# A pipelined convolution, attention and mixture-of-experts kernel: transposes of z moved on TensorE, rank sums from 5 products in place of 14

## The reference, cut to what matters

```
x = x + conv(_gn(x))          # a 7x7 filter per image and channel, made from the image: keys, softmax,
                              # 1x1 conv, layer norm, relu, 1x1 conv; then the depthwise convolution
t = tokens(x)                 # (16, 256, 128)
z = _ln_t(t)
q = tanh(z);  a = softmax(q q^T / sqrt(128));  t = t + a z
z2 = _ln_t(t)
probs = softmax(z2 router_w + router_b);  the best 2 of 8 experts per token
t = t + sum over the 2: prob * expert(z2)       # 128 -> 256 -> gated 256 -> 128
```

## Time and profile before

| | |
|---|---|
| Median of 3 runs | 386.15 us (382.89 to 387.73) |
| Profiled execution, its own time | 386.41 us |
| Its span | 384.6 us |
| TensorE busy in the span | 302.8 us (79%) |
| VectorE, ScalarE, GpSimd busy | 236.7, 132.4, 164.2 us |
| Mean granted TensorE clock | 0.87 of full speed |
| First phase, to the end of GpSimd's last row DMA | 239.9 us |

### The profile page before, as it was taken

How to read it: one execution, slowest core, us unless ns; L and a number is a source line. 1 busy time by engine, 2 the same in 40 slices (tenths; PEclk the granted TensorE clock), 3 DMA queues, 4 the chain that set the end, 5 groups by cost and what they waited for, 6 DMA issues and landing times.

```text
span 384.6 us, 7449 instructions
## 1 busy us (share of the span) xinstructions
PE 302.8 (79%) x1731; PEld 239.7 (62%) x1732; DVE 236.7 (62%) x1006; ACT 132.4 (34%) x443; POOL 164.2 (43%) x187
## 2 busy tenths in 40 slices
PE   1686989998989899998876661599999999999200
PEld 1264667786868777777664440388878787888100
DVE  2433475488887877676866652266666676666164
ACT  0312221425152515141303012266656565666000
POOL 3000010030256565555455577046656566666400
PEclk9958896999999999989887655599999999999755
DMA  7722241221523000101010013223332322231197
GB/s 221 250 80 67 84 125 28 85 68 30 182 79 97 31 30 21 38 21 37 22 35 29 29 56 107 55 80 81 85 94 84 89 77 83 80 93 59 48 322 288
DMA packets 29945, 33.37 MB, mean 87 GB/s; under 512 B 5096, under 2 KB 23740, under 8 KB 29658
## 3 DMA queue, kind: packets, MB, share of 16 engines
q1 hardware_dynamic: 23312, 22.00, 18.9%
q0 software_dynamic: 4384, 8.60, 6.7%
q10 hardware_dynamic: 2218, 2.42, 1.8%
HBM read 21.76 MB, written 11.75 MB: 87 GB/s over the span
## 4 chain that ended last, share of the span: by engine, by line
PE 44%; issue 21%; POOL 21%; DMA 5%; DVE 4%; SPq 3%; ACT 1%; POOLq 0%; DVEq 0%; ACTq 0%
POOL rows_dram L410 15%; PE bank L1324 8%; PE bank L1312 5%; PE bank L1307 5%; PE bank L1308 5%; PE bank L1317 4%; PE bank L833 3%; DMA w_high<-moe_dram 2%; PE bank L876 2%; POOL ln_rstd L437 2%; PE bank L1302 2%; SPq L1160 2%; PE bank L978 2%; POOL ln_rstd L433 2%; PE bank L914 1%
## 5 line engine op out<-in xcount | busy, mean ns | idle before, releaser
L1132 POOL DMA_INDIRECT moe_dram<-ys,xs x72 | 70.4, 978 | 51.2 <-issue 30.8
L410 POOL DMA_INDIRECT rows_dram<-row,slot x64 | 62.7, 979 | 18.2 <-issue 18.2
L1324 PE MATMUL bank<-w_all,gatedt 128*128 x288 | 44.1, 276 | 0.2 <-ACT gatedt L1175 0.2
L1249 DVE SCALAR_TENSOR_TENSOR ys<-b_all,xs,bank 128x128 f32<-128x128 f32 x72 | 25.0, 347 | 28.5 <-issue 27.0
L1259 DVE SCALAR_TENSOR_TENSOR gated<-bank,xs,silu 128x256 f32<-128x256 f32 x72 | 34.8, 483 | 10.2 <-ACT silu L1183 7.8
L1183 ACT ACTIVATE silu<-bank 128x256 f32<-128x256 f32 x72 | 27.6, 383 | 35.7 <-PE bank L1312 35.7
L1324 PEld LDWEIGHTS bank<-w_all,gatedt 128*128 128x128 f32 x288 | 38.0, 192 | 0.4 <-issue 0.4
L1307 PE MATMUL bank<-w_high,x_high 128*128 x72 | 35.6, 494 | 0.0
L978 PE MATMUL bank<-zhat,const 121*128 121x256 f32 (+1 forms) x128 | 31.2, 399 | 0.0
L1312 PE MATMUL bank<-w_high,x_low 128*128 x72 | 30.3, 421 | 0.7 <-issue 0.7
L423 POOL TENSOR_TENSOR frstd<-fvar,minus_half 128x2 f32<-128x2 f32 x8 | 5.7, 708 | 57.5 <-DVE fvar L703 57.5
(11 more groups left out here) (172 smaller groups left out, 593.7 us busy)
## 6 DMA issues: line engine op xcount, KB each, us to landing
xs<-rows_dram SPq DMA_DIRECT2D x72, 66.0 KB, 1.8
xc<-in_x SPq DMA_DIRECT2D x8, 256.0 KB, 2.9
wgv<-in_wg SPq DMA_DIRECT2D x8, 256.0 KB, 2.9
wgv<-in_wv SPq DMA_DIRECT2D x8, 256.0 KB, 3.4
xt<-in_xt SPq DMA_DIRECT2D x4, 512.0 KB, 4.6
xt<-moe_dram SPq DMA_DIRECT2D x8, 256.0 KB, 6.0
w_high<-moe_dram SPq DMA_DIRECT2D x8, 256.0 KB, 6.6
out<-w_high ACTq DMA_DIRECT2D x8, 256.0 KB, 5.6
```

The source lines that it names most:

```text
L410: pool.indirect_dma_start(rows_dram, bass.IndirectOffsetOnAxis(ap=slot[:, f % 2, 2 * t + k:2 * t + k + 1], axis=0), row[:, f % 2, t, k, :] ...
L1132: pool.indirect_dma_start(moe_dram, bass.IndirectOffsetOnAxis(ap=xs[:, u, C + 1:C + 2].bitcast(U32), axis=0), ys[:, u, :], None, bounds_ch ...
L1324: last = pe.matmul(bank_y[v][:, 0:C], gatedt[:, v, h * P:(h + 1) * P], w2_all[:, bass.ds(e * (2 * C) + h * C, C)], start=(h == 0), stop=(h ...
```

## The change

Three edits. First, in rounds with stages B and D (4 to 9) `features_of_z` moves ahead of the mean of the filters and of `features_spectrum`, and ScalarE's tanh moves ahead of both `ghat` copies. Second, from round 9 on (the rounds after stage A's last) the rows' transposes go to `bank_k` in place of `bank_t`; they then wait for `fraw_done` and the `z2t` copy of the round before, not for `gt_done` and `qt_done`. In the rounds without stage B (10 to 12) they are also put ahead of the scores, where before they stood behind. Third, the ranks of the four tiles and the totals come out of one accumulation over 40 columns: one product with `before` over all of `either`, which has a fifth tile of zeros now, and four with `ones`, each of one tile's columns repeated over all later tiles. That is 5 products in place of 14 (4 with `before`, 6 and 4 with `ones`).

```diff
-        either = sb("either", [P, TILES, EXPERTS], BF16)
+        either = sb("either", [P, TILES + 1, EXPERTS], BF16)
...
+        rounds_of_a = PAIRS + A
+
+        def z2t_bank(i):
+
+            return bank_t if i < rounds_of_a else bank_k
...
-                    act.activation(z2t[:, :], bank_t[:, :], ACT.Copy).then_inc(z2t_done, 1)
+                    act.activation(z2t[:, :], z2t_bank(i)[:, :], ACT.Copy).then_inc(z2t_done, 1)
...
+                    if d is not None:
+
+                        act.wait_ge(zt_psum, d + 1)
+                        after(act, score_psum, 2 * d)
+                        act.activation(qt[:, :], bank_t[:, :], ACT.Tanh).then_inc(qt_done, 1)
                     if b is not None:
 
                         act.wait_ge(ghat_psum, 2 * b + 1)
...
-                    if d is not None:
-
-                        act.wait_ge(zt_psum, d + 1)
-                        after(act, score_psum, 2 * d)
-                        act.activation(qt[:, :], bank_t[:, :], ACT.Tanh).then_inc(qt_done, 1)
...
                     pe.wait_ge(z2_done, e + 1)
-                    after(pe, gt_done, through(i, A))
-                    after(pe, qt_done, through(i, D))
+                    if i < rounds_of_a:
+                        after(pe, gt_done, through(i, A))
+                        after(pe, qt_done, through(i, D))
+                    else:
+                        pe.wait_ge(fraw_done, PAIRS)
+                        after(pe, z2t_done, through(i - 1, E))
...
+                    if d is not None and b is not None:
+
+                        features_of_z(i, d)
                     if b is not None:
 
                         pe.wait_ge(f0_done, b + 1)
...
-                    if d is not None:
+                    if d is not None and b is None:
                         features_of_z(i, d)
-                    if e is not None and b is not None:
+                    if e is not None and (b is not None or a is None):
                         router_input(i, e)
...
-                    if e is not None and b is None:
-
-                        router_input(i, e)
-                        router(i, e)
-                    if e is not None and b is not None:
+                    if e is not None:
                         router(i, e)
...
-                        for t in range(TILES):
-                            for u in range(t):
-                                pe.matmul(bank_b[:, 64 + t * EXPERTS:64 + (t + 1) * EXPERTS], ones[:, :], either[:, u, :], start=(u == 0), stop=False)
-                            pe.matmul(bank_b[:, 64 + t * EXPERTS:64 + (t + 1) * EXPERTS], before[:, :], either[:, t, :], start=(t == 0), stop=True)
+
+                        ranks = bank_b[:, 64:64 + (TILES + 1) * EXPERTS].rearrange("p (t e) -> p t e", e=EXPERTS)
+                        pe.matmul(ranks, before[:, :], either[:, :, :], start=True, stop=False)
                         for u in range(TILES):
-                            last = pe.matmul(bank_b[:, 96:96 + EXPERTS], ones[:, :], either[:, u, :], start=(u == 0), stop=(u == TILES - 1))
+                            last = pe.matmul(ranks[:, u + 1:, :], ones[:, :], spread(either[:, u, :], 1, TILES - u),
+                                             start=False, stop=(u == TILES - 1))
                         last.then_inc(rank_psum, 1)
```

More of the change, by code:

```diff
@@ L448, in _, with router_input @@
                 act.wait_ge(ld_c1, 32)
-                def router_input(e):
+                def router_input(i, e):
                     act.wait_ge(z2t_psum, e + 1)
                     after(act, logit_psum, e)
-                    act.activation(z2t[:, :], bank_t[:, :], ACT.Copy).then_inc(z2t_done, 1)
+                    act.activation(z2t[:, :], z2t_bank(i)[:, :], ACT.Copy).then_inc(z2t_done, 1)
                     act.activation(row[:, e % 2, :, 1, 0:C], row[:, e % 2, :, 0, 0:C], ACT.Copy).then_inc(row2_done, 1)
@@ L505, in _ @@
                     if e is not None and b is not None:
-                        router_input(e)
+                        router_input(i, e)
                     if d is not None:
@@ L548, in _ @@
                 dve.memset(ones[:, :], 1.0)
+                dve.memset(either[:, TILES, :], 0.0)
                 def layer_norm_stats(src, raw, mv, var, stats_step, var_done, p):
@@ L705, in _ @@
                         dve.wait_ge(route_step, 7 * e + 3)
-                        dve.tensor_tensor(either[:, :, :], chosen[:, :, 0, :], chosen[:, :, 1, :], ALU.add).then_inc(either_done, 1)
+                        dve.tensor_tensor(either[:, 0:TILES, :], chosen[:, :, 0, :], chosen[:, :, 1, :], ALU.add).then_inc(either_done, 1)
                     if e is not None:
@@ L840, in router_input @@
                     pe.wait_ge(z2_done, e + 1)
-                    after(pe, gt_done, through(i, A))
-                    after(pe, qt_done, through(i, D))
+                    if i < rounds_of_a:
[4 more added lines that the diff above has]
+                        after(pe, z2t_done, through(i - 1, E))
                     for t in range(TILES):
-                        last = pe.transpose(bank_t[:, t * P:(t + 1) * P], row[:, e % 2, t, 0, 0:C], ident)
+                        last = pe.transpose(z2t_bank(i)[:, t * P:(t + 1) * P], row[:, e % 2, t, 0, 0:C], ident)
                     last.then_inc(z2t_psum, 1)
```

## The result

The changed kernel takes 390.97 us (median of 4 runs, 389.52 to 394.37), the kernel before 384.52 (4 runs, 381.81 to 387.73); the ratio is 1.0211, 95% interval [1.012, 1.0302]. Timed again beside three experiments on another chip the ratio was 1.0185 [1.0111, 1.0259]. Ratios leave out disturbed executions of either kernel; the medians quoted are of all. The profiled execution took 389.52 us against 386.41 before. So the change costs 3 us in the profiled pair and 8 and 7 us by the two ratios, with lower ends of 4.6 and 4.3; the forecast was 390.5, which is 4.1 more than the profiled execution of before. The kernel before and after spend 144.75 and 143.90 us behind GpSimd's last row DMA, so the second phase is 0.85 us shorter.

A forecast was written before the change was run, and what follows sets the result against it. TensorE was taken to bound steady rounds, and the start of `ln2_rstd` of pair 7 to decide the first phase. Terms + 3.9 + 4.3 - 3.0 - 1.1 = +4.1 us on 386.41 gave 390.5, range 386 to 395.

The forecast's parts named there:

- The instant: End of first phase: the start of `ln2_rstd` of pair 7 alone decides it; forecast 4.1 us later.
- the sum: At `ln2_rstd` of pair 7: + 3.9 + 4.3 - 3.0 - 1.1 = +4.1 us.
- Edit 1: Rounds 5 to 9, z transposed early: 0.60 us a round gained, 3.0 us in all, bounds 2.0 and 3.9.
- the push by the moved transposes: Round 8 on TensorE: z's transposes, moved ahead, push the transform back by 0.57 us.
- that cover: Round 8: rows ready at 149.61, transposes want them at about 150.1, so 0.5 us to spare.
- Edit 3: Ranks in rounds 5 to 8 and 11: 9 fewer products save 0.22 us a round, 1.1 us in all.
- Edit 2: Rounds 10 and 11: scores queue behind transposes waiting for VectorE's rows, costing 3.9 and 4.3 us.
- (a): Rounds 10 and 11: scores don't wait, gains come whole, 382.3 us; chance 0.10 for 381 to 384.
- (b): Rounds 10 and 11: low clock slows transform back and router, + 3.6 us, 394.1; chance 0.13 for 394 to 397.
- (c): Rounds 5 to 9: another wait binds the scores, gain 0 to 1, time 392.5 to 393.5; chance 0.12.
- The rule on strict order of matmuls: TensorE: matmuls start and end in program order, only weight loads go ahead; the opposite rule would give 382.3 us.

The follow-up runs named there:

- after_again: The changed kernel itself, unaltered, timed again on another chip: 392.66 us beside 389.31 for the kernel before, ratio 1.0185.
- rows_first: Kernel before, with the rows' transposes ahead of the scores in rounds 10 to 12, still in `bank_t`: 399.49 us beside 389.31, ratio 1.0173.
- z_early: Kernel before, with z transposed ahead of the transform in rounds 4 to 9 and tanh ahead of both `ghat` copies: 384.96 us beside 389.31, ratio 0.9958.
- scores_first: Changed kernel, with the scores back ahead of the rows' transposes in rounds 10 to 12: 382.28 us beside 389.31 for the kernel before, ratio 0.9835.
- rows_in_gap: scores_first, with GpSimd sending pair 6's first tile (2 row DMAs) before its round 11 wait for `ln2_var`: 418.30 us beside 417.47 for the kernel before, ratio 1.0023.

## Why the prediction was right, and where it wasn't

**The instant.** Forecast + 4.1 us for `ln2_rstd` of pair 7, measured + 3.93; 390.5 us forecast, 390.97 measured. The order of events was as forecast, and attention of pair 7 came 8.6 us later counted from z's transposes of round 10 (forecast 8.2). The nearness of the numbers is in large part luck. The 3.93 us are a sum in which the clock has terms as large as the edits' own: 0.15 to the start of round 3, + 3.89 in round 3, - 3.52 in round 4, - 5.23 in the early segment, + 3.49 in round 10, + 5.15 in round 11. The first three, 0.52 together, have almost nothing to do with the change (0.2 of round 4 is edit 1). And 390.5 stands on the profiled 386.41, while the median of before came out at 384.52.

**The size in whole times.** The ratios put the loss at 8 and 7 us, and the lower ends of their intervals, 4.6 and 4.3, lie above the forecast difference of 4.1. So the loss was under-forecast. The granted clocks on record point to the term: the profiled execution of before ran at 0.870, while its five quickest beside after_again ran at 0.886 or 0.887. Both profiled executions of the changed kernel were the quickest of their sets. The traced pair therefore understates the loss, and more of it than the traces show may be the clock, the term that the sum put at nothing. In which rounds the longer executions lose it no trace shows.

**Edit 1, 3.0 us in five rounds.** The size for a round was a little low and the count of rounds wrong: the changed kernel has four at 0.70, and 0.2 more in round 4. Round 5 took 20.36 us (80.62 to 100.98) against 21.28 (80.10 to 101.38), which is 0.92 less, 0.22 of it ranks and so 0.70 the edit, not 0.60. I had taken 0.57 us as the push by the moved transposes; their pitch ahead of the mean is 0.50 (144.53 to 145.03). Round 9 gave 0.03: the rows' transposes wait 0.75 us for VectorE's rows there. I had checked that cover, 0.5 us, in round 8 and carried it to round 9, where stage A is gone and TensorE is there sooner. In sum, edits 1 and 3 gave 102.54 - 99.01 = 3.5 us up to round 10 at equal clock, against 3.9 forecast. The 5.2 in the profiled pair hold 1.7 of clock.

**Edit 3, 0.22 us a round.** As forecast: from the first product to the end of the last it is 0.27 us, against 0.49. In round 7 the chain through GpSimd and `gbuf` took back 0.18 of it: the round was shorter by 0.74, not 0.92.

**Edit 2, the waits.** The mechanism was right in both rounds: the pause, its releaser and what is queued behind. Round 10 lost 3.5 to 4.1 us in the two traces of the changed kernel against 3.9 forecast, and 2.8 to 3.4 against the mean of the old order. The scores started 0.3 us later than forecast, as the transposes took 1.11 us. The scores themselves took 2.90 us in place of 3.65, the clock having risen, so that the router followed after 4.32 us and not after 5.07. Round 11 lost 5.15 against 4.3 less the ranks' 0.2. This term was mis-sized by the clock: the router took 1.88 us in place of 1.06, and the rows' transposes 1.12 in place of 0.66.

**Rivals.** Rows ready in time (a): refuted by the pauses. The clock (b): real, some 1 us in round 11 of the changed kernel and 2 us in round 10 of rows_first, but no full 3.6 in the profiles. In other executions it isn't excluded: 394.1 was its time, and single executions of the changed kernel reached 394.37 and 393.67. No gain from edit 1 (c): refuted by z_early's segments.

**The rule on strict order of matmuls.** The experiments bear out what the Trainium skill's page "TensorE: Matmul & The Clock Gate", section "The mechanism", says of it. In round 10 of rows_first the scores' operand was ready at 191.93 us, yet the scores started at 196.23, behind transposes that waited until 195.33.

## What to carry to other kernels

An instruction that is moved forward in an in-order queue brings its wait along. Ask of each position not whether the operation could be done there but when its last operand arrives, and do it in every round in which the set of stages differs: here the same early position is free in rounds 5 to 8, costs 0.75 us in round 9 and 4 us in rounds 10 and 11. When whole times scatter by more than the effect, cut the traces at the same instructions and compare the segments, and look at the granted clock in each before you put a difference down to an edit. The version to keep is scores_first, 1.1 to 1.7% faster than the kernel before.

## What the hardware did that I had not expected

The same kernel took 417.47 us on one chip and 389.31 and 386.00 on two others. Most of the excess lies in the second phase: in rows_in_gap there it lasts 165.2 us, from the last row DMA's end at 249.83 to the span's end, against 144.8 in the trace of before, and in the other three traces of that chip 171 to 173. The 72 DMAs that send the blocks back are as long as before (70.4 us together), the idle time of GpSimd ahead of them is 71.6 us in place of 51.2. The cause stays open.

TensorE's granted clock also falls without a long pause: in round 7 of rows_first the 16 matmuls of the transform back took 6.82 us, against 3.71 at full clock, after no pause longer than 0.78 us. The mean granted clock there (140.45 to 147.20) was 0.53. Such falls come in some executions and not in others. From round 5 on each is worth 1.7 to 3.1 us, and in round 3 it made 3.9 us between the two profiled executions, as much as any single edit here.
